# A mixture-of-experts layer computed on all tokens instead of on routed tiles

## The reference, cut to what matters

```python
x = x + L0_xattn(ln(x), ctx)     # 16 heads
x = x + L0_ffn(ln(x))            # 8 experts, top 2, hidden 512, gelu
x = x + L1_xattn(ln(x), ctx)     # 1 head, biases
x = x + L1_ffn(ln(x))            # 8 experts, top 2, hidden 256, relu, biases
x = x + L2_xattn(ln(x), ctx)     # 16 heads of 64, mask: query i sees key i alone
x = x + L2_ffn(ln(x))            # quantised, ternary weights, conv of 3 taps, silu
x = x + L3_xattn(ln(x), ctx, mask)
x = x + L3_ffn(ln(x))            # 8 experts, top 2, 2 x 512, silu(g) * u

# L1_ffn, the part that is changed:
logits = xf @ Wr + br
topk_w, topk_idx = top_k(logits, 2);  topk_w = softmax(topk_w)
gate = sum(one_hot(topk_idx, 8) * topk_w[..., None], axis=1)       # (t, 8), six are 0
h = relu(einsum('th,ehf->etf', xf, W1) + b1[:, None, :])           # f = 256
y = einsum('etf,efh->eth', h, W2) + b2[:, None, :]
out = einsum('te,eth->th', gate, y)
```

## Time and profile before

| what | us |
|---|---|
| median of 3 executions | 761.67 (761.16 to 762.99) |
| the profiled execution's own time | 763.77 |
| its span, first to last instruction | 762.0 |
| layer 0's MoE slots | 113.4 to 203.5 |
| layer 1's attention, norm, routing | 203.5 to 298.6 |
| layer 1's MoE slots | 298.6 to 367.9 |
| second combine, keys and values, set-ups | 367.9 to 396.2 |
| third attention and quantisation of x | 396.2 to 446.9 |
| `ffn2` | 446.9 to 505.7 |
| fourth attention, routing | 505.7 to 597.5 |
| last MoE and output | 597.5 to 762.0 |

### The profile page before, as it was taken

One profiled execution on the slowest core, in us unless ns is written; L12 is line 12 of the kernel. 1 busy time (PEld: TensorE's weight loads), 2 busy tenths in 40 slices (PEclk: granted clock), 3 DMA queues, 4 the chain that ended last, 5 costly groups with the idle time before them and its releaser, 6 DMA issues.

```text
span 762.0 us, 13194 instructions
## 1 busy us (share of the span) xinstructions
PE 551.9 (72%) x3830; PEld 472.1 (62%) x3845; DVE 356.6 (47%) x1306; ACT 240.0 (31%) x615; POOL 306.9 (40%) x415
## 2 busy tenths in 40 slices
PE   4998439999742535999864169959980599999930
PEld 2676319999632534989522147737770599999930
DVE  6788830001509745001249948887787022222232
ACT  1453005555310101655310023425420233333310
POOL 6000277648360162969450000000005777457634
PEclk9998559999955555999985569969965599999985
DMA  9930013324210010444110070030001122122222
GB/s 281 301 119 2 14 59 93 92 76 107 80 49 0 10 54 27 123 113 128 49 38 2 16 219 1 0 111 1 1 1 38 53 77 70 43 57 73 59 65 62
DMA packets 74485, 52.65 MB, mean 69 GB/s; under 512 B 9339, under 2 KB 67620, under 8 KB 74285
## 3 DMA queue, kind: packets, MB, share of 16 engines
q1 hardware_dynamic: 68301, 39.58, 18.0%
q0 software_dynamic: 6144, 12.60, 5.9%
HBM read 32.71 MB, written 19.43 MB: 68 GB/s over the span
## 4 chain that ended last, share of the span: by engine, by line
PE 53%; DVE 19%; issue 17%; another core or an unknown queue 4%; POOL 4%; DMA 2%; SPq 1%; ACT 1%; POOLq 0%; DVEq 0%; ACTq 0%
PE bank L1612 21%; PE bank L1626 14%; PE bank L1445 5%; PE bank L1600 2%; POOL XNR L553 2%; PE bank L1533 2%; PE bank L1502 2%; DVE XNR L804 2%; DVE stats L780 1%; POOL YG L553 1%; PE bank L1522 1%; PE bank L1565 1%; DVE X L1002 1%; DVE minus_half_vyy L798 1%
## 5 line engine op out<-in xcount | busy, mean ns | idle before, releaser
L539 POOL DMA_INDIRECT xs<-XNR,slot_i x96 | 94.2, 981 | 264.8 <-DVE slot_i L962 243.4
L1612 PE MATMUL bank<-xT,wcur 128*128 128x128 f32 x1288 | 179.7, 285 | 1.2 <-issue 0.4
L1612 PEld LDWEIGHTS bank<-xT,wcur 128*128 128x128 f32 x1288 | 164.3, 198 | 5.7 <-issue 2.1
L987 DVE TENSOR_TENSOR hT<-gb,bank 128x512 f32<-128x512 f32 x46 | 31.7, 688 | 109.0 <-ACT gb L647 109.0
L1002 DVE SCALAR_TENSOR_TENSOR X<-XNR,gates,X 128x128 f32<-128x128 f32 x48 | 14.3, 370 | 133.0 <-DMA XNR<-ys,slot_i 133.0
L571 POOL COPY wcur<-WA 128x512 f32 x92 | 56.4, 616 | 20.9 <-PE bank L1612 18.3
L553 POOL DMA_INDIRECT XNR<-ys,slot_i x48 | 47.1, 982 | 34.9 <-DMA ys<-Y 23.6
L1600 PE MATMUL bank<-ident,xrow 128*128 128x128 f32 x138 | 39.4, 289 | 26.4 <-DMA xrow<-xs 16.0
L647 ACT ACTIVATE hT<-bank 128x512 f32<-128x512 f32 (+1 forms) x92 | 45.1, 491 | 41.1 <-issue 16.4
L553 POOL DMA_INDIRECT YG<-ys,slot_i x48 | 48.1, 1001 | 11.1 <-issue 10.7
L655 ACT ACTIVATE Y<-bank 128x128 f32<-128x128 f32 x138 | 38.3, 278 | 42.2 <-PE bank L1626 30.5
(11 more groups left out here) (311 smaller groups left out, 1044.3 us busy)
## 6 DMA issues: line engine op xcount, KB each, us to landing
xrow<-xs SPq DMA_DIRECT2D x138, 64.0 KB
ys<-Y SPq DMA_DIRECT2D x138, 64.0 KB
WA<-in_fc_dram SPq DMA_DIRECT2D x16, 256.0 KB, 4.4
xs<-zeros SPq DMA_DIRECT2D x2, 1472.0 KB, 10.5
WA<-in_pj_dram SPq DMA_DIRECT2D x8, 256.0 KB, 6.0
WB<-in_fc_dram SPq DMA_DIRECT2D x8, 256.0 KB, 4.6
WB<-in_pj_dram SPq DMA_DIRECT2D x8, 256.0 KB, 6.6
xs<-XNR,slot_i POOLq DMA_INDIRECT x96
```

The costliest lines, as they stand in the source:

```text
L539: pool.indirect_dma_start(out=xs_dram[g], out_offset=bass.IndirectOffsetOnAxis(ap=slot_i[:, k, t:t + 1], axis=0), in_=XNR[:, t, :], in_off ...
L987: dve.tensor_tensor(hT[s][:, :, :], gb[s % 2][:, :, :], bank[2 + s % 2][:, :].rearrange("p (c t) -> p c t", c=4), ALU.mult).then_inc(ex_mu ...
L1612: ins = pe.matmul(dst, wcur[:, s4, at:at + P], xT[s4 % 2][:, :], start=True, stop=not L["bias"])
```

## The change

The MoE of layer 1 has no routing to DRAM any more. The 2048 tokens are 4 blocks of 512, and each block meets each of the 8 experts: 32 units `u`. In a unit TensorE spreads the expert's gate over all partitions (one bf16 matmul of 512 columns, `sel` against the turned gates `gT`), does two up products of 512 columns (fp32) and the two down products of the unit before (`dense_down`); ScalarE copies the gates to `gB` and does two Relu with the bias as operand (`b1c`); GpSimd multiplies the two hidden chunks by `gB` (`gate_products`). The down products of a block pile up in one bank, with the biases b2 as three bf16 matmuls ahead of them. The result has tokens in the free direction; it is copied, turned back (`dense_rows`) and added to X (`add_dense`).

The two halves are `dense(0)` and `dense(1)`. A table says after which unit of a half a piece of other work stands in TensorE's order: in `dense(0)` the second half's transposes, attention, norm, logits and gate rows; in `dense(1)` the third attention on the first half of the batches. The third attention on the second half stands in steps 0 to 3 of `ffn2`, where VectorE also quantises that half's x (`quantise_x(1, ...)`, 6 tiles and then 2). `ffn2` has a ring of three banks instead of four, turns x at steps 4 and 5 for the last two sequences, and makes the mask at step 6 instead of 2. The second half of layer 0's rows is combined after the gates of the first half. Keys and values of the third attention are made before the first scores, and those of the fourth attention in layer 0's routing (`setup3` between the two `ranks`; GpSimd's `keys3` before its scatter).

```diff
+    dict(up=512, f=512, act=ACT.Gelu),
+    dict(up=1024, f=512, act=ACT.Silu),
 ]
+BLOCKS = GT // BT
+DSTEPS = BLOCKS * E
+DCHUNKS = 2
+UPRING = 3
+S_T2, S_SC, S_T3, S_LG, S_GT = 4, 5, 10, 11, 14
+X_T, X_Q, X_O = 3, 4, 7
+assert X_O + 1 == E
+X2B = (7, 3)
+F2XB = (6, 3)
...
+            load_down(in_dense, DOWN1, pj1)
+            sp.dma_start(b1c[:, :, :].rearrange("f e c -> f (e c)"),
+                         bias_in[0:E * 256].rearrange("(e f) -> f e", f=P),
+                         allow_slow_non_contiguous=True).then_inc(in_dense, 16)
...
-            experts(1)
...
+            sp.wait_ge(x2_added, 2)
...
+            def gate_products(g):
+                for u in range(g * DSTEPS, (g + 1) * DSTEPS):
+                    pool.wait_ge(d_gc, u + 1)
+                    for c in range(DCHUNKS):
+                        n = u * DCHUNKS + c
+                        pool.wait_ge(d_relu, n + 1)
+                        h = hT[n % RING][:, :, :].rearrange("p c t -> p (c t)")
+                        pool.tensor_tensor(h, h, gB[:, u % 2, :], ALU.mult).then_inc(d_mul, 1)
             link(pool.memset(score_rows[:, :, :], 0.0))
...
+            keys3()
             experts(0, [UP0])
             pool.wait_ge(ex_dn, SLOTS)
             pool.memset(cb[:, :].bitcast(F32), 0.0).then_inc(cb_clear, 1)
             gather(1, 0, MOVES)
-            pool.wait_ge(in_rows, 48)
-            experts(1, [UP1])
+            for g in range(GROUPS):
+                gate_products(g)
+            experts(1, [GATE3, UP3])
             gather(3, 0, MOVES)
-            experts(2, [GATE3, UP3])
-            gather(5, 0, MOVES)
...
+            def dense(g, side):
+                for u in range(g * DSTEPS, (g + 1) * DSTEPS):
+                    act.wait_ge(d_gb, u + 1)
+                    if u >= 2:
+                        act.wait_ge(d_mul, (u - 1) * DCHUNKS)
+                    act.activation(gB[:, u % 2, :], bank[3][:, :], ACT.Copy).then_inc(d_gc, 1)
+                    for c in range(DCHUNKS):
+                        n = u * DCHUNKS + c
+                        act.wait_ge(d_up, n + 1)
+                        if n >= RING:
+                            act.wait_ge(d_dn, n - RING + 1)
+                        act.activation(hT[n % RING][:, :, :].rearrange("p c t -> p (c t)"), bank[n % UPRING][:, :], ACT.Relu,
+                                       bias=b1c[:, u % E, c:c + 1]).then_inc(d_relu, 1)
+                    for piece in side.get(u - g * DSTEPS, ()):
+                        piece()
...
+            def gates_by_expert(g):
+                flat = [P, GT, E]
+                dve.wait_ge(lg1_mm, g + 1)
+                top_two(bank[6][:, 0:GT * E].rearrange("p (t e) -> p t e", e=E), br_all[:, :])
+                dve.tensor_tensor(de[:, :], m2[:, :], m1[:, :], ALU.subtract).then_inc(top_ready, 1)
+                dve.wait_ge(e2_ready, g + 1)
+                link(dve.tensor_scalar(den[:, :], e2[:, :], 1.0, None, ALU.add))
+                link(dve.reciprocal(pr1[:, :], den[:, :]))
+                link(dve.tensor_tensor(pr2[:, :], e2[:, :], pr1[:, :], ALU.mult))
+                dve.tensor_tensor(oh1[:, :, :], oh1[:, :, :], pr1[:, :].unsqueeze(2).broadcast_to(flat), ALU.mult)
+                link(dve.tensor_tensor(oh2[:, :, :], oh2[:, :, :], pr2[:, :].unsqueeze(2).broadcast_to(flat), ALU.mult))
+                link(dve.tensor_tensor(place[:, :, :], oh1[:, :, :], oh2[:, :, :], ALU.add))
+                dve.wait_ge(gparts_clear, 1)
+                if g:
+                    dve.wait_ge(gt_mm, g)
+                split3([gparts[:, :, i * E:(i + 1) * E] for i in range(PARTS)], place[:, :, :]).then_inc(parts_ready, 1)
             def products():
                 def multiply(t, s):
...
+            def ffn2(side):
                 def x_low(b):
                     dve.wait_ge(f2_xh, b + 1)
-                    dve.tensor_tensor(xql[:, b % 2, 1:S + 1], bank[6][:, :], xqh[:, b % 2, 1:S + 1].bitcast(F32),
+                    if b == 0:
+                        for t in (xqh, xql):
+                            dve.memset(t[:, :, 0:1].bitcast(F32), 0.0)
+                            dve.memset(t[:, :, S + 1:S + 2].bitcast(F32), 0.0)
...
                 x_low(0)
+                x_low(1)
                 def pair_stats(p):
                     for i in (2 * p, 2 * p + 1):
@@ -1201,13 +1353,15 @@
                     return ins
                 for p in range(TILES // 2 + 2):
-                    if p % 2 == 0 and p // 2 + 1 < B:
-                        x_low(p // 2 + 1)
+                    for b in F2TURNS.get(p, ()):
+                        x_low(b)
                     if p >= 2:
                         add(p - 2)
                     if p < TILES // 2:
                         quantise(p)
-                    if p == 2:
+                    for piece in side.get(p, ()):
+                        piece()
+                    if p == 6:
                         dve.wait_ge(in_mask3, 16)
...
                 router(0, g)
+            keys1()
+            values(bank[7], lambda: dve.wait_ge(v3_mm, 1), v3_ready)
+            query_bias_rows()
             setup1()
             XN0, XN1 = XNR[:, 0:GT, :], XNR[:, GT:TILES, :]
             combine(0)
             layer_norm(half(0), XN0, xn_ready)
+            softmax1_top(0)
             weight_sums()
-            attention1_softmax(0)
+            softmax1_share(0)
+            ternary_weights()
+            attention1_add(0)
+            layer_norm(half(0), XN0, xn_ready)
+            weight_taps()
+            gates_by_expert(0)
...
             combine(1)
-            attention1_add(0)
-            layer_norm(everything, XNR[:, :, :], xn_ready)
-            router(1, 0)
-            attention1_softmax(1)
+            layer_norm(half(1), XN1, xn_ready)
+            softmax1_top(1)
+            softmax1_share(1)
             attention1_add(1)
             layer_norm(half(1), XN1, xn_ready)
-            router(1, 1)
-            combine(GROUPS)
-            keys(1)
-            mean_value()
-            masked_result()
-            dve.wait_ge(s2_evac, 2)
+            gates_by_expert(1)
+            add_dense(0)
             split_taps()
-            combine(GROUPS + 1)
-            xattn2()
-            ffn2()
+            add_dense(1)
+            x2_rows(0)
+            x2_scores(0)
+            x2_mix(0)
+            x2_add(0)
+            quantise_x(0, 0, BT)
+            add_dense(2)
+            add_dense(3)
+            x2_rows(1)
+            ffn2({1: [lambda: x2_scores(1)],
+                  2: [lambda: x2_mix(1), lambda: quantise_x(1, 1, BT - 1)],
+                  3: [lambda: x2_add(1), lambda: quantise_x(1, 0, 1)]})
             attention(1)
             for g in range(GROUPS):
-                router(2, g)
+                router(1, g)
             products()
             for g in range(GROUPS):
-                combine(2 * GROUPS + g)
+                combine(GROUPS + g)
...
+            def dense_down(u):
+                block, e = u // E, u % E
+                y = bank[4 + block % 2][:, :]
+                if e == 0:
+                    if block >= 2:
+                        pe.wait_ge(d_added, block - 1)
+                    at = block % BLOCKS * 512
+                    for i in range(PARTS):
+                        pe.matmul(y, b2p[:, i, :], gT[:, block // BLOCKS, at:at + 512], start=(i == 0), stop=False)
+                for c in range(DCHUNKS):
+                    n = u * DCHUNKS + c
+                    pe.wait_ge(d_mul, n + 1)
+                    last = e == E - 1 and c == DCHUNKS - 1
+                    ins = pe.matmul(y, DOWN1[:, e, c * P:(c + 1) * P], hT[n % RING][:, :, :].rearrange("p c t -> p (c t)"),
+                                    start=False, stop=last)
+                    ins.then_inc(d_dn, 1)
+            def dense(g, side):
+                pe.wait_ge(gt_ready, g + 1)
+                for u in range(g * DSTEPS, (g + 1) * DSTEPS):
+                    block, e = u // E, u % E
+                    at = block % BLOCKS * 512
+                    if u:
+                        pe.wait_ge(d_gc, u)
+                    pe.matmul(bank[3][:, :], sel[:, e:e + 1].broadcast_to([P, P]), gT[:, g, at:at + 512],
+                              start=True, stop=True).then_inc(d_gb, 1)
+                    for c in range(DCHUNKS):
+                        n = u * DCHUNKS + c
+                        if n >= UPRING:
+                            pe.wait_ge(d_relu, n - UPRING + 1)
+                        pe.matmul(bank[n % UPRING][:, :], UP1[:, e, c * P:(c + 1) * P],
+                                  XT[:, block * BT:(block + 1) * BT, :].rearrange("p t c -> p (t c)"),
+                                  start=True, stop=True).then_inc(d_up, 1)
+                    if u:
+                        dense_down(u - 1)
+                    for piece in side.get(u - g * DSTEPS, ()):
+                        piece()
+            def dense_rows(i):
```

(75 more changed lines are left out.)

651 lines of the change are left out of this document (364 added, 287 removed).

## The result

The changed kernel took 766.97 us (median of 9 runs, 766.07 to 767.52) beside 760.48 for the kernel before (9 runs): ratio 1.0086, interval 1.0064 to 1.0108. It is slower by 0.9%, where 3% less was forecast, and it lies above the range of 727 to 763 us. Its profiled span is 764.8 us at a mean granted clock of 0.861 (before: 762.0 at 0.810).

What follows compares the result with a forecast made beforehand. TensorE was taken to bound layer 1's slots, VectorE's chains or waits the stages around. 238 + 140.4 + 8 + 97 = 483.4 against 505.7 (−22.3), −1 ahead: −23.3; forecast 738 us, 8-in-10 range 727 to 763.

Steps and rivals of the forecast that it cites:

- From 203.5 to the first unit: Layer 0's last slot to the first dense unit: scores at 207.6, first unit at about 238 us.
- rival B: Late semaphore or cold clock again before the dense part: first unit at 245 to 257, time 745 to 757; chance 0.20.
- Ahead of the slots: Moved set-up (setup3, keys3) before layer 0's slots: −1 us, ends −1 and +2.5, the scatter covering most of TensorE's part.
- The first half's chain: After layer 0's slots: scores, softmax to products (8.2 us), norm (6.9), taps, gates and turning, first unit about 238.
- Half clock: Ahead of the first unit: transposes, keys, values and logits slower at clock 0.5; +4 us taken, between 0 and +10.
- The units: Layer 1's dense part: 32 units 117.1, side pieces 17.8, late clock 3.5, stalls 2; sum 140.4 us.
- Rival C: GpSimd's gate multiply bounds the dense units: gain gone at 2.2 us each, about 795 at 3.0; chance 0.09.
- The FFN: Ternary FFN with half the third attention and quantisation added: +38 us on 58.8, so 97.
- The rest: From the fourth attention's first transposes (505.7 us) on: nothing is changed.
- rival E: TensorE stays at half clock in the dense part: unit 7.3 us, time about 855; chance 0.03.
- D: FFN work is cheaper: half of 28.8 + 9 falls into existing waits, 10 less, 728; chance 0.10.
- the terms behind the dense part: End of dense to the FFN's first product: copy, turn, add, `x2_rows(1)` 5.2, first x 0.8; given as 8 us.

Runs made afterwards that it cites:

- e1_hold: Changed kernel with GpSimd's 16 second-half gathers held back until the first half's attention was added to X; 764.05 us, ratio 1.0083 to the kernel before.
- e10_before: The kernel before, unaltered, profiled on a chip without late updates; span 746.8 us.
- e0_after: The changed kernel, unaltered, on a chip without late updates; 750.19 us, ratio 1.0013 to the kernel before.
- e4_keys: Changed kernel with keys3's four masked multiplies taken from GpSimd and made by ScalarE as 16 scaled copies; 763.73 us, ratio 1.0093.
- e3_rows: Changed kernel with VectorE's split of the query bias rows after setup1's copies, awaited only before the first down product; 763.75 us, ratio 1.0082.
- the chip of the pair: Chip without late updates where the kernel before and the changed kernel were both profiled unaltered; spans 746.8 and 750.8 us.
- e8_three: Changed kernel with gathers in two runs of eight, bias rows split behind setup1's copies, keys3's masked multiplies on ScalarE; 751.24 us, ratio 1.0043.
- e17_three: Changed kernel with the 64 gate multiplies on VectorE, bias rows split behind setup1's copies, keys3's masked multiplies on ScalarE; 780.90 us, ratio 1.0318.
- e7_split: Changed kernel with the sixteen gathers in two runs of eight, the second after the first half's attention was added to X; 750.96 us, ratio 1.0039.
- e14_split: The changed kernel with gathers in two runs of eight, same program run once more on the same chip; span 751.3 us.
- e11_first: Changed kernel with first-half logits and gates ahead of the taps, mean_value and masked_result moved into the dense part; 754.90 us, ratio 1.0085.

## Why the prediction was wrong

**The failed step** is in "From 203.5 to the first unit". The wait at the scores, which had lasted to 227.23, was taken out ("the scores come at 207.6"), and nothing was put into the sum for late updates behind it; rival B, at 0.20, kept them outside. The scores themselves came as said: 5.1 us after the slots' end, forecast 4.1. But where updates are late, the wait came back behind the next product of TensorE, 11.7 us of the stretch's +15.6, and 4.9 us more ahead of the slots. Where they are not late, the kernel before lacks them as well and is 15.2 us faster. So some 14 of the 23 us of gain (8.1 at the scores, 5.5 beside the second scatter) were lateness of the kernel before: on one chip it moves to another place, on another it was never there. Of the 26.1 us by which the span missed, 14.0 are what the changed kernel's two profiles differ by. That the lateness goes with the gathers is shown by e1_hold, and that it is not on every chip by e10_before and e0_after; why some chips have it, by nothing here.

**Ahead of the slots** (−1, with +2.5 as the worse end): mis-sized by 7.6 us, 2.7 without late updates. "The scatter covers most of TensorE's part" forgot VectorE: a norm stretched by GpSimd's keys3 (2.1 us, shown by e4_keys) and bias rows split in front of setup1's copies (4.2 us of work, 2 at the slots in e3_rows). Both edits at once gave 2.3 us where updates are on time (e8_three) and 4.0 where they are late (e17_three). The other 4.9 are late updates beside the scatter, by the pair of rows above.

**The first half's chain without late updates.** From the slots' end the forecast has 4.1 us to the scores, 8.2 to the end of the addition, 6.9 of norm and 15.3 to the first unit, 4 of these for half clock. On the chip of the pair the same four were 5.5, 10.2, 7.1 and 15.7, which is the +3.8 together with slots 0.2 shorter. Half clock was priced right: the gates' wait of 5.2 us is within the 15.3, and the clock's share measured about 4 (e7_split and e14_split). The miss is in softmax, shares and products, 2.0 us, and in the scores, 1.4.

**The units** (117.1, side pieces 17.8, clock 3.5, stalls 2, then 8.0): off by 5 us in 148. The size of TensorE's work was near (139.6 us busy; clock 0.98, better than assumed). The stalls were mis-sized: TensorE's side pieces waited 6.5 us for VectorE where 2 were put in, and 8 us in all come from the meeting of GpSimd and VectorE. Rival C had the right pair of engines and the wrong victim: the multiply stayed at 1.29 us on average, far from the 2.2 of its break-even, and VectorE's operations paid. (1.2 was assumed; the estimate of 1.1 us was too low.)

**The FFN** (97): 95.2 to the first transposes of the fourth attention. Right, with VectorE busy 66 us, a little under the 70 named as the mark. 36 us of the 50.7 that the third attention and its quantisation took before came back here, forecast 38.

**The rest** (no change) came out as said, and rival E (half clock in the dense part) did not come. Three slips of arithmetic changed nothing here: half of D's 28.8 + 9 is 19 us and not 10; the ends of the range, 727 and 763, are not D's 728 and B's 757; the terms behind the dense part add up to 7.8, not 8.0.

## What to carry to other kernels

A wait that the profile can't name is not a gain until it is known what makes it: compare a second chip, or hold back the suspect, before it goes into a sum. When work moves to GpSimd, price VectorE's operations beside it, the smallest first: here each of those held up lasted up to 1.19 us instead of 0.17, nearly the 1.27 of GpSimd's own operation. And work moved from an idle stage into one that TensorE bounds costs its full length there (e11_first: 6.4 us more of busy time, 6.5 of the stretch).

## What the runs showed of the hardware

- Semaphore updates of TensorE arrived up to 11.7 us late (224.4 to 236.1) beside GpSimd's gathers on two chips at least, and on time on two others, with the same program and the same pace of gathers; VectorE's updates to itself came up to 1.2 us late beside the scatter. The kernel before differs by 9 us between them (757.0 and 748.2).
- An operation of VectorE on 8 columns took 0.17 us alone and 1.13 us beside GpSimd's two-input multiply, one of two inputs and 1024 columns 1.22 and 2.29; the statistics of the layer norm stayed at 0.28, and GpSimd's multiply at a median of 1.27.
- One program on one chip had a clock of 1.00 or of 0.52 in the same 5 us between the slots and the first unit, and the first unit 4.1 us apart.
